# One drive operation over two PSUM banks, issued between two scans of the unit before

## The reference

```python
def step(h, ins):
    dt_t, B_t, C_t, x_t = ins
    dA = jnp.exp(dt_t[:, :, None] * A)
    h = dA * h + dt_t[:, :, None] * B_t[:, None, :] * x_t[:, :, None]
    y = jnp.einsum('bdn,bn->bd', h, C_t)
    return (h, y)
```

## Time and profile before

| | |
|---|---|
| median of three runs | 2926.74 us (2926.32 to 2929.57) |
| profiled execution | 2924.0 us; its span, first to last instruction, 2922.3 us |
| mean granted TensorE clock over the span | 0.914 of full speed |
| state-space units on VectorE, first drive to last scan | about 1960.9 to 2902.8 us |
| VectorE busy over the whole span | 2039.8 us (70%) |

### The profile page before, as it was taken

The page is one execution under the profiler, slowest core; times in us unless marked ns, Lnnn a source line. Parts: engine busy times, 40 slices in busy tenths (PEclk is TensorE's granted clock), DMA queues, the critical chain, the costliest instruction groups (busy, mean ns, idle before and its releaser), DMA issues.

```text
span 2922.3 us, 38854 instructions
## 1 busy us (share of the span) xinstructions
PE 2550.3 (87%) x12408; PEld 1263.1 (43%) x12408; DVE 2039.8 (70%) x4256; ACT 1658.4 (57%) x3091; POOL 1218.0 (42%) x1356
## 2 busy tenths in 40 slices
PE   7879899999999998899999987867888888888865
PEld 4555423223233232288888876722222222222222
DVE  7689688788798885011111115528999999999997
ACT  4631466666666667733333343357867767768662
POOL 4330112221221222200000008428988879888885
PEclk9999999999999999999999998978789798797777
DMA  6677323314133221155555567435656566666563
GB/s 214 195 164 187 110 41 54 64 36 65 37 63 52 41 43 29 31 180 196 192 191 192 186 238 220 157 78 151 172 152 177 150 168 178 153 178 165 150 171 94
DMA packets 217255, 388.19 MB, mean 133 GB/s; under 512 B 56777, under 2 KB 154060, under 8 KB 212060
## 3 DMA queue, kind: packets, MB, share of 16 engines
q1 hardware_dynamic: 210908, 368.90, 46.9%
q0 software_dynamic: 6144, 16.82, 1.8%
HBM read 303.69 MB, written 81.96 MB: 132 GB/s over the span
## 4 chain that ended last, share of the span: by engine, by line
PE 49%; DVE 23%; issue 9%; ACT 7%; POOL 4%; DMA 2%; another core or an unknown queue 1%; POOLq 0%; SPq 0%; DVEq 0%; ACTq 0%
PE ps L1816 48%; DVE hh L1789 8%; DVE mp L1594 6%; POOL Ch L978 3%; DVE ps L1776 3%; ACT Pt L1132 2%; DVE ps L1591 1%; ACT dA L1330 1%; DMA dA<-step_rows 1%; PE ps L2021 1%; PE ps L2045 1%; DVE zs L1798 0%; ACT te L1280 0%; ACT te L1283 0%
## 5 line engine op out<-in xcount | busy, mean ns | idle before, releaser
L1132 ACT ACTIVATE Pt<-ps 128x512 f32<-128x512 f32 (+3 forms) x1280 | 594.2, 547 | 277.9 <-PE ps L1816 261.3
L1594 DVE TENSOR_REDUCE mp<-ps 128x1 f32<-128x512 f32 (+3 forms) x1152 | 644.3, 596 | 62.4 <-PE ps L1816 45.5
L1816 PE MATMUL ps<-qk 99*128 99x512 bf16 (+7 forms) x2560 | 589.9, 359 | 49.7 <-DVE mp L1594 23.6
L978 POOL TENSOR_TENSOR Ch<-hh,Cb 128x1024 f32<-128x1024 f32 x256 | 604.5, 2363 | 45.2 <-DVE hh L1789 45.2
L1789 DVE TENSOR_TENSOR_SCAN hh<-dA,hst,ps 128x512 f32<-128x512 f32 x384 | 473.1, 1272 | 0.0
L854 POOL TENSOR_SCALAR_AFFINE_SELECT Pt<-Pt 128x128 f32<-128x128 f32 x512 | 145.8, 293 | 751.5 <-ACT Pt L1132 741.1
L1816 PEld LDWEIGHTS ps<-qk 96*128 96x128 bf16 (+1 forms) x2560 | 218.0, 99 | 513.0 <-DVE mp L1594 232.7
L1330 ACT ACTIVATE dA<-dA,A 128x512 f32<-128x512 f32 x512 | 337.9, 713 | 151.8 <-DMA dA<-step_rows 149.3
L1776 DVE TENSOR_TENSOR ps<-ps,Bb 128x512 f32<-128x512 f32 x512 | 327.6, 689 | 62.2 <-PE ps L1816 61.0
L1644 DVE TENSOR_TENSOR yb<-ps,b2b 128x256 f32<-128x256 f32 x71 | 30.2, 425 | 420.0 <-PE ps L1816 420.0
L1816 PE MATMUL ps<-Pt,vg 128*32 128x512 f32 (+3 forms) x2560 | 310.0, 558 | 9.1 <-POOL Pt L854 5.4
(11 more groups left out here) (312 smaller groups left out, 2963.0 us busy)
## 6 DMA issues: line engine op xcount, KB each, us to landing
dA<-step_rows SPq DMA_DIRECT2D x256, 512.0 KB, 4.7
we<-in_experts SPq DMA_DIRECT2D x39, 2052.0 KB, 7.8
qk<-qk_parts SPq DMA_DIRECT2D x192, 128.0 KB, 5.1
qk_parts<-q SPq DMA_DIRECT2D x32, 384.0 KB, 3.0
expert_out<-yb SPq DMA_DIRECT2D x32, 257.0 KB, 8.8
expert_in<-zero SPq DMA_DIRECT2D x32, 256.0 KB, 3.8
xg<-expert_in SPq DMA_DIRECT2D x32, 256.0 KB, 2.7
step_rows<-dt SPq DMA_DIRECT2D x128, 64.0 KB, 3.5
```

Of the source, the lines that this page charges most:

```text
L978: pool.tensor_tensor(Ch[:, k % 6, :, :], hh[:, k % HRING, :, :], Cb[:, par:par + 1, :].broadcast_to([P, 2, CH]), ALU.mult).then_inc(s_Ch, 1)
L1132: act.activation(Pt[:, n % PRING, q0:CH], ps[:, score_bank(n, plan), q0:CH], ACT.Exp, scale=SCALE).then_inc(s_exp, 1)
L1594: ins = dve.tensor_reduce(part, slot[:, 0:plain], AX.X, ALU.max)
L1816: return pe.matmul(o, lhsT, rhs, start=start, stop=stop, **kw)
```

## The change

The two operations of a drive become one over both banks, with B repeated by a stride of zero. `s_Bu` then counts units and not tiles. On VectorE the drive of unit k + 1 moves up: it stands behind the first scan of unit k (and behind `gate_y`, where there is one), ahead of the second scan of unit k. The first drive of all stays in front of the loop. Nothing is changed on the other engines but the count for which ScalarE waits before it overwrites B.

```diff
                 if m > 1:
-                    act.wait_ge((s_Bu, s_Ch)[w], (2, 1)[w] * UNITS * (m - 1))
+                    act.wait_ge((s_Bu, s_Ch)[w], UNITS * (m - 1))
...
                 dve.wait_ge(s_dxb, k + 1)
-                for a in range(2):
-                    b = ps[:, 2 * (k % XRING) + a, :]
-                    dve.tensor_tensor(b, b, Bb[:, par, :], ALU.mult).then_inc(s_Bu, 1)
+                b = ps[:, 2 * (k % XRING):2 * (k % XRING) + 2, :]
+                dve.tensor_tensor(b, b, Bb[:, par:par + 1, :].broadcast_to([P, 2, CH]), ALU.mult).then_inc(s_Bu, 1)
...
-                dve.wait_ge(s_Bu, 2 * k + a + 1)
+                dve.wait_ge(s_Bu, k + 1)
...
                 n, u = divmod(k, UNITS)
-                drive(k)
+                if k == 0:
+                    drive(0)
                 scan(k, 0)
                 if u in (11, 19, 27):
                     gate_y(n, u // 8 - 1)
                 if n and u == 3:
                     gate_y(n - 1, KI - 1)
+                if k + 1 < NC * UNITS:
+                    drive(k + 1)
                 scan(k, 1)
```

## The result

The change makes the kernel slower: 2987.98 us median (2983.4 to 2991.96) against 2927.47, a ratio of 1.0207, 95% interval 1.0195 to 1.0219; 60.5 us more, where 54 had been worked out and 2978 forecast. The profiled execution took 2991.96 us (span 2990.2), the longest of the four. Its state-space units run on VectorE from 1962.4 to 2969.2 us (first drive to the end of the last scan), 1006.8 us against 941.9 before (1960.90 to 2902.8): 65 us more in this stage.

What follows compares the result with a forecast made beforehand. VectorE's instruction pace was taken to bound the stage. From the profiled 2924 us, - 15.7 (merge) - 21 (today's waits) + 51 (bare wait) + 40 (backlog) = + 54 gave 2978 us; range 2936 to 3025.

Steps and rivals of the forecast that it cites:

- The bound: State-space stage: it runs at the pace of VectorE's instructions, so changes to them count in full unless VectorE must wait.
- old waits: VectorE's waits within the stage today, for TensorE at drives and for decays, fall away: 21 us off.
- The merge: VectorE's drive: one 1.222 us operation, 1.12 start to start against 1.17 for two; 0.06 us a unit, 15.7 us off.
- The bare wait: Even units' drives wait for a spread even if TensorE is free: 0.18 us full clock, 1.13 half clock; 51 us added.
- The backlog: Spreads starting late because TensorE is still at earlier work, hidden before, are now paid at VectorE's drives: 40 us added.
- surplus: Late-spread waits at u = 4, 28, 0 and 30: 3.0 us a chunk, 18 over six; 7 more for places in one chunk or two.
- the catch-up: ScalarE works off its lateness at u = 22 to 26, so the wait around u = 28 is 0.6, not 2.7 us.
- it stays: TensorE's work behind u = 3 does not wait for ScalarE, so the 2.2 us wait around u = 4 remains.
- the first: Rival: banks are ready by the time the moved drive is due, only the merge's gain remains; 2908 us, chance 0.04.
- Only the bare wait: Rival: TensorE and ScalarE use the longer pairs to work off all backlog; 2938 us, chance 0.15.
- The clock: Rival: TensorE waits more often and its granted clock falls; 3053 us at half clock, 3015 half-way, chance 0.15.
- 41 us: Merge's gain on VectorE if the next operation starts only once the pipeline empties, 0.16 us a unit; prediction kept 0.06.

Runs made afterwards that it cites:

- without spreads: Changed kernel with TensorE's spreads left out and drives taking the minimum instead of the product: 2912.27 us; the kernel before, cut the same way: 2908.56 us.
- The move alone: Against the kernel before: a drive stays two operations, both moved between the two scans of the preceding unit; 2999.47 us, ratio 1.0247.
- the odd units alone: Against the kernel before: only odd units' drives merged and moved, even units' two operations left in their old place; 2940.34 us, ratio 1.0044.
- single spreads: Changed kernel, but TensorE spreads one unit at a time, unit k + 3 as soon as unit k is scanned; 2955.39 us, ratio 1.0113.
- the job bank first: Changed kernel, ScalarE emptying the job bank ahead of step-size operations: 2987.6 us with one TensorE projection moved to step 2, 2987.11 us without.

## Why the prediction held, point by point

*The bound.* VectorE's pace with its waits sets the stage: 65 us more of stage are the forecast's terms with their measured sizes, - 15.9 (merge) - 21 (old waits) + 98 (new waits at drives) + 3 (a decay) = + 64. The 98 are 88.6 of idle time and 0.10 of lost overlap at each of 92 waits; counted from start to start, with 24 shorter waits too, the drives come 100 us late.

*The merge.* Right: 1.219 us, 1.12 start to start, 0.062 a unit. The order of operations by itself costs nothing, as the unit of 3.47 without spreads shows. What I had not seen is that the merge needs the move: in the old place it costs 36 us.

*The bare wait.* Right in place and size: 0.09 of idle time and 0.10 of overlap at full clock (0.18 forecast), 1.04 and 1.12 idle in the half-clock stretch (1.13 with the overlap forecast), none under the gate of u = 11 in the full chunks. The move alone and the odd units alone show that this is the loss's place, and single spreads take the wait away where TensorE has time.

*The backlog.* The term that was mis-sized. The 100 us can be split: a spread of the length that it had, started as soon as its scan ended, accounts for 50 of them (51 forecast), and the other 51 are spreads that started late (40 forecast). In the second to seventh chunk lateness costs 4.6 to 7.1 us, 36 in all, where 18 of surplus and 7 for single places had been set; in the first it is 10 (13 forecast), in the last 4 (2 forecast). The forecast's places repeat (u = 4, 28, 30 and 0), but there are more of them: the drives of units 4, 8, 14 and 20 come to 14 us in the six chunks. That of unit 14 (u = 12) had 0.6 to 0.8 in each, and its spread is 0.48 to 0.60 late in the kernel before too; that of unit 4 had 0.4 to 0.8 in five, under a gate that the forecast let cover it. At u = 28 the wait was 0.6 to 1.6 (0.6 forecast, 2.7 without the catch-up, a figure for which the prediction shows no working; its 0.45 should be 3.88 - 3.47 = 0.41). ScalarE did catch up: TensorE's waits for it there, before and after:

```profile
PE ps L1816 <- ACT dt L1272: 6.2, 6, 1.0
```
```profile
PE ps L1818 <- ACT dt L1272: 0.2, 1, 0.2
```

At u = 4 the wait was 0.6 to 3.6, 1.9 in the mean (2.2 forecast), and here the mean hides what decides. The work was TensorE's own, as predicted, but its length is not fixed. The first matmuls of it in the third and the fourth chunk, the drive of unit 6 in the third (for the fourth, see 2365.18 above), and windows over both places:

```profile
2235.73 2.08 PE L1818 MATMUL ps<-xs,Dd 128*128 128x512 f32 x2 [2.54 <-DVE hh L1788]
```
```profile
2360.00 1.12 PE L1818 MATMUL ps<-xs,Dd 128*128 128x512 f32 x2 [2.54 <-DVE hh L1788]
```
```profile
2242.43 1.23 DVE L1775 TENSOR_TENSOR ps<-ps,Bb 128x1024 f32<-128x1024 f32 x1 [2.11 <-PE ps L1818]
```
```profile
2235.70:2242.40 6.70, 6.63 (x22) 1.69 (x22) 4.62 (x4) 4.00 (x6) 5.68 (x5) 0.76 0.99 278
2360.00:2365.20 5.20, 5.11 (x22) 1.45 (x22) 4.62 (x5) 2.28 (x4) 4.06 (x2) 1.00 1.03 287
```

In the two chunks with a granted clock of 1.0 there the wait was 0.58; in the four with 0.61 to 0.76, half clock for a part of the place, it was 2.1 to 3.6. The move alone shows the same split: 0.51 and 0.52 at 1.0, 2.1 to 2.35 at 0.75. The rows that the forecast of 2.2 was read from the earlier trace rows lie in a stretch with a clock of 0.75, so "it stays" held only where that clock stayed.

*The rivals.* The wait bites at once, so the first is out. "Only the bare wait" is out by the late spreads. The clock of the second to seventh chunk did not fall as a whole (0.84 to 0.89 after, 0.84 to 0.88 before), and all spreads together take as long as before:

```profile
L1818 PE MATMUL ps<-dtx,pick 32*128 32x512 f32 x1024 | 182.9, 778 | 40.6 <-DVE hh L1788 40.6
```

So the rule of the Trainium skill, page "TensorE: Matmul & The Clock Gate", section "HAM oscillation", did not decide the time of the stage, though the last chunk, with 0.64 after 0.68, agrees with its direction. The stretch from 2430 to 2452, at 0.50, is the one that was at half clock before. Operations of VectorE overlap after the change too: a scan starts at 2431.26, before the drive of 2430.15 + 1.21 has ended. The Trainium skill, page "VectorE: DVE Perf Modes", section "The DRAIN you can't avoid", does not speak against this, as the prediction has it: the section goes on: "A next op that is not held starts earlier". The overlap of 0.10 agrees with that sentence, so 41 us was not what the section as a whole would give.

## What to carry to other kernels

Before an operation is moved up in its engine's order, ask what releases its input and count the instructions between that release and its new place: work that was hidden by 3.5 us of distance was bare at 1.1. A merge of two operations paid its fixed cost back here only where the operation that needs the result did not follow at once. And where two engines hand banks back and forth, a moved operation shifts the release of everything behind it, so a bound that was not the tightest (the gate, the emptying of the job bank) can take the gain back. Where equal places wait unequally, compare the granted clock at each of them: here it parted 0.6 us from 2.1.

## What the runs showed of the hardware that was not expected

A VectorE operation that waits for the one right ahead of it on the same engine started 1.34 us after that one, 0.13 behind its end, where an operation that does not depend on it started after 1.12: 0.22 us lost each time. Profiled executions of the same earlier stages differed by up to 9 us in when the first drive began (1960.90 before, 1969.7 with the job bank first), though no instruction ahead of it had changed; single profiles of this kernel are not to be compared to a few us by their end.
